# A kernel of eight layer stages on one core: two heads' outputs per column group, one tile for two ternary tails, and a new order of all parts

## The chip, the core and the metric

The kernel runs on one core of a Trainium2 chip, as one program. The metric is the device time of a launch in microseconds. TensorE multiplies, VectorE (DVE) and ScalarE (ACT) do arithmetic and are the only ones that read its results from the accumulation banks, POOL does arithmetic and some DMA issues, and SyncE (SP) issues DMAs. There are eight banks of 128 partitions by 512 fp32 columns.

## What is computed

x has 16 blocks of 128 tokens by 256 features. Eight sub-layers follow one another, each `x = x + f(layernorm(x))`: an attention of 32 heads of 8 dimensions with rotary positions (stage 0 in the code), a product-key expert lookup (1), a grouped attention (2), a routed mixture of experts (3, with 8 and 9 for its tiles), an attention of 16 heads (4), a ternary feed-forward (5), a wide attention of 16 heads of 128 (6) and a feed-forward in blocks of 8-bit numbers (7). The change touches stages 0 and 5:

```
stage 0:  q = rope(x Wq), k = rope(ctx Wk), v = ctx Wv;  P = softmax(q k^T / sqrt(8));  out = (P v) Wout + bout
stage 5:  tern(w) = clip(round(w / s), -1, 1) * s,  s = mean |w|     (w1, w3: 682 x 256, w2: 256 x 682)
          out = (silu(x tern(w1)^T) * (x tern(w3)^T)) tern(w2)^T
```

## The kernel before

All engines work block by block, and several blocks and two stages are under way at once. Each engine's program is a fixed list of parts. `STEPS` names the steps of a stage, how many parts each has per block and which engines take part; `ORDER` (lines 74 to 142) holds for each engine one letter per part, and `timetable` (line 258) turns the letters into the order. `BANKS` says which of the eight banks a step fills; a bank is taken in the order of TensorE's list, and `room` (line 920) makes TensorE wait until the last user of that bank has been read. So the letters and the banks together set who waits for whom.

Stage 0, one block, on TensorE (`small_heads`, line 938; s is 0 for this stage and 4 for the third attention, which shares the code): xT (transpose of the normalised block), qk and vp (projections), tqk (transposes of q and k), mx (four parts: scores, for their row maximum, which VectorE takes at L1881), tq2, st (four parts: transposed scores), pv (eight parts, L1036), tb (L1046), oT (L1053, L1054) and out (L1061, L1062). Scores are products with 32 rows, so they run on quarters of the array. ScalarE takes the exponential of four heads at a time (step ex, L1469) and pv multiplies them by v. v is kept as 32 columns a head in `u0.vt`, of which 8 hold v, one holds 1.0 (its product is the softmax sum) and the others 0.0. The four heads of a part go to four groups of 32 columns of the array, so to four groups of 32 partitions of the bank:

```
h = 16 * (c // 4) + 4 * j + c % 4
r = slice(E * j % 128, E * j % 128 + E)
k = (c - c0) * (E // 32) + E * j // 128
```

Parts 0 to 3 fill bank oa and parts 4 to 7 bank ob. ScalarE copies each out (step ot, L1476, 128x512), TensorE transposes each back in four pieces (step tb, banks ra and rb), and VectorE divides by the sum (step norm, a reciprocal at L1892 and a product at L1896, for 16 heads each). Then oT transposes the 256 features (L1483 on ScalarE copies them) and out multiplies by Wout; VectorE adds to x at L1767. The banks: oa and ra are bank 7; ob and rb are bank 2, which also takes tk. `pv_gone` (line 717) tells ScalarE when a buffer of exponentials is free again.

Stage 5 (`ternary`, line 1252): the weights are turned into -1, 0, 1 in bf16 at the start (step tp on VectorE, L2240 to L2264); x is split into three bf16 parts (step sp), so each product is three. Step h has two parts per block: part 0 fills banks h1 and h3 with tiles 0 to 3 of 128 hidden features, part 1 with tiles 4 and 5, where tile 5 has the last 42 features. Each tile takes 6 products (L1268): 72 in all per block. ScalarE takes silu of h1 (L1635, and L1637 and L1638 for part 1), VectorE multiplies by h3 (L2281, L2284, L2285), the result is split again (step gs) and multiplied by w2 (step out, L1277).

Stage 3's step rk (line 1181) ranks tokens for their expert: `lowh` times this block's marks plus `oneh` times the running sum `seen`, which VectorE writes.

Of the kernel before, what the change touches and what calls it, by code (L numbers as in the profile page):

```python
# [9 lines left out]
BF16 = mybir.dt.bfloat16  # L10
# [3 lines left out]
ALU = mybir.AluOpType  # L14
# [61 lines left out]
        "Zeeaabaababaccdbadbaddfdgdbadhhgdhhgcighfdhhhegdbihgdjhhghkdcaigfdhhhhedbigdahgjhdhkhcigfdhghhdbhgdaihghehdghcjgfdhh"  # L76
        "kdihhegbihdghachjghdkghifdhhhegdibhghadhghcgdjhhhhfikdiebdgahjdghkhgdchgfdhhhhedigibghahhdghjcgdkhhhhfdiiedgbgjhhhdk"
        "ghcgdlhhhhfiidegbdjghhkhgdhcgidlhhhhefidmdgbjghhdhkghdcgilfdhhhhdgiehdgjcdhhghkdgifhdhhhegdihghchjgdhkgdifhhdhhegdih"
        "ghchjgdhkgdifhhdhhgedihghdhjgnhkgfihhhhgoiomghonjhhghhhkigmhhoppiojonokplopmqppnloopomorplnpqpmpooowponwpqrpoopopowp"
        "qrploowomppwnoplqwpowompplonopmqpplnmopoonqoplpoomponolmpnxpqpoopopolqpmpoonopopxqplpomonpooplqpoomopnpopxqplooopmop"  # L80
        "npxqxppwooopxpoqppoossoxpptstopqxptsrspptsuttsqtsrsvuutsvuvvutstsrutsvutsyvutstsvvztstsCuAutsBvutyvzvsutrusCvAtsvruu"
        "BtsvvtuuvysrtzsvuutsAtsvBtsCuvvytzusuvutstsrvCutsAvvuuvttssyutBsrvzuytvCvAusrtuBtsszvuCtsAtvuyvuvBsztyszurvuAtstvutv"
        "vuCsAsytBuvzuBsvCurvAuvtstystBsrtuCtvzusstAtvusvvtuBsyutrsstCtszvutvAuvvuBsyutCszstvuvutvvAusCsytztuBvuAvuvCuBvsstyt"
        "zsusttCvuAvuvvuuBvyuzvuCvvAIBJIIJKJKIyJzIKJIIKJAKCJBDKKEEFEFEFGFEGHFEGHEFEHGFEGFEHHGFEGFEHHGFEGFEHHGFEGFEHHGFEGHFEGH"
        "FEGHFEGFEHHGFEGFEHHGFEGHFEGHFEGFEHHGFEGFEHHGFEGFEHHGFEGFEHHGFEGFEHHGFEGFEHHGFEGFHHGFGHGHGHHIIJJIIKJIKJIKLJIKJOMKJIIK"
        "JKJLKLMOKLMNPNMPQNRQSSSSTPOTLNURMVPQSSSSTORQLTSSTLNUMSSROMVPTLSSLTUNVQPMSSOTRLNSSSSQPTOMTURQUSSVTLNSSROTSSVPTNUQSSPO"
        "MLTRVMUSSLMTLSSOQTVRUNSSLMTPSSNOQPMTZZZZRVNSSQPUTZSSNOTMLRQVSSPSSTNORUTMSSSSQPOTTWWRUQSSVNSSRTONPWSXSTSSQPOXVQRUTTXW"
        "YWXWXWXUSSSSTRXWXYXWSSXYTYSSXVXUTTYVXWXVYUXWXUXWYVXXVXXWYYWXWYXXXXYXXXXW61Y6YXY6XY06Y62062626110-1-1-321321032132415"
        "324154153231421534235241543251342531-41245-450332152-401533724211354253421835014315223424517384525435143224598815+43"
        "2513417501923841528323011234+4557124385984351+424132951527130+843524851432145530129213+13212473578415248403253512435"  # L90
        "891834+5424235597213104+53288403542114232519157321831+48534254234113257507421539881+342541241353251984+3053184715425"
        "4252878793234+5389843754854+8984558+9788+9+9+"),
    "V": (
        "aahabbaababbcaabacbacbaddeebceebaceebaeeaeeeebeecaeedfeeeefeecgeedfieebjeeafeebceegidfjeeeeeebcfeedeegefeicfjeebdeeg"
        "ifeeeefceedeefgeeifeeceegeedyeeeeffceedeegeefeefceegdeejffeeeecgeedfeejfeeeeceegeedfeeeefeedeegeefeeeefdeegeefeeeefd"
# [220 lines left out]
def program(nc, A, out):  # L316
    with ExitStack() as ctx:
# [2403 lines left out]
```

## Time and profile before

| | us |
|---|---|
| median of 3 runs | 2075.73 (2074.39 to 2076.0) |
| the profiled execution | 2073.72 |
| its span, first to last instruction | 2071.8 |
| TensorE busy | 1968.2 (95%) |
| VectorE busy | 1684.7 (81%) |
| ScalarE busy | 1276.6 (62%) |
| granted TensorE clock, mean of the span | 0.990 |

An engine's busy time is the union of its instructions' durations. TensorE's products are pipelined: one has a duration of 0.27 us or so, while the next starts after a part of that, so the mean of a row is a latency and the busy time divided by the count is nearer to its price. PE is the product, PEld the loading of the fixed operand. An fp32 product stands as two records, a transpose as one. Stage 0 lies at about 0 to 240 us, stage 1 to about 590, stage 4 at about 1110 to 1380 and stage 5 at 1297 to 1434.

### The profile page before, as it was taken

What the parts mean: (1) busy time and instruction counts of PE and PEld (TensorE: products, weight loads), DVE (VectorE), ACT (ScalarE), POOL (GpSimd) and SP (SyncE); (2) the same over time, 40 slices, a digit from 0 to 9 for tenths busy, and PEclk for the clock granted to TensorE, in tenths of its full rate; (3) what the DMA queues carried; (4) which work ended last, traced back from release to release, by engine and by line L of the source; (5) the groups of instructions that cost most, each with busy time, mean ns of one, the idle gap of its engine ahead of it and who ended that gap; (6) DMA issues with size and microseconds to landing.
All of it is one profiled execution on the core that took longest, in us unless ns stands there. A gap on an engine that the chain in (4) does not pass through costs nothing.

```text
span 2071.8 us, 46041 instructions
## 1 busy us (share of the span) xinstructions
PE 1968.2 (95%) x16038; PEld 1533.0 (74%) x16038; DVE 1684.7 (81%) x4558; ACT 1276.6 (62%) x3230; POOL 779.6 (38%) x1160
## 2 busy tenths in 40 slices
PE   5999999999999999998998999999899999999998
PEld 3666799899988888887987777887465566555656
DVE  6777899999789997766555788896788988888887
ACT  2778988888855455444654666644666566646661
POOL 7332030000012232222117887022877556646640
PEclk8999999999999999999999999999999999999999
DMA  9400210000045353432211120033667454545540
GB/s 343 140 2 3 78 52 2 2 2 2 13 139 192 113 169 97 133 115 74 91 65 37 29 68 2 2 126 121 223 211 226 133 167 154 186 149 183 170 127 28
DMA packets 223518, 215.75 MB, mean 104 GB/s; under 512 B 25926, under 2 KB 197992, under 8 KB 222264
## 3 DMA queue, kind: packets, MB, share of 16 engines
q1 hardware_dynamic: 197048, 129.17, 20.6%
q0 software_dynamic: 26240, 83.65, 11.2%
q8 instruction: 128, 2.10, 0.4%
q14 instruction: 102, 0.84, 0.1%
HBM read 115.73 MB, written 96.99 MB: 103 GB/s over the span
## 4 chain that ended last, share of the span: by engine, by line
PE 50%; DVE 24%; POOL 8%; issue 7%; DMA 5%; ACT 3%; SPq 3%; DVEq 0%; POOLq 0%; ACTq 0%
PE pb L1135 3%; PE pb L1268 3%; PE pb L1158 3%; PE pb L1107 3%; PE pb L1091 3%; PE pb L1036 3%; PE pb L1009 3%; SPq L873 2%; PE pb L1216 2%; PE pb L1143 2%; PE pb L1150 2%; PE pb L1207 2%; PE pb L1277 2%; PE pb L1100 1%; DMA turn3k<-areaA 1%
## 5 line engine op out<-in xcount | busy, mean ns | idle before, releaser
L2462 POOL TENSOR_SCALAR sm<-sm 128x1 f32<-128x1 f32 x128 | 33.5, 262 | 457.9 <-DVE sm L1752 457.3
L1517 ACT ACTIVATE areaB<-i128h,workB 128x128 f16<-128x128 f16 x512 | 156.3, 392 | 0.9 <-DVE workB L1997 0.6
L1544 ACT ACTIVATE workA<-workA 128x128 f32<-128x128 f32 x256 | 99.5, 390 | 64.0 <-DVE workA L2044 63.8
L1680 ACT ACTIVATE workA<-pb,workA 128x128 f32<-128x128 f32 x256 | 113.8, 457 | 34.5 <-DVE workA L2343 33.0
L1325 PE MATMUL pb<-areaA,workA 128*128 128x256 f32 x512 | 121.7, 382 | 3.8 <-ACT workA L1671 3.7
L1091 PE MATMUL pb<-areaB 128*128 128x128 f32 x1024 | 124.7, 277 | 0.3 <-ACT workB L1507 0.3
L1135 PE MATMUL pb<-xT,areaA 128*128 128x128 f32 x1024 | 124.7, 276 | 0.0
L1135 PEld LDWEIGHTS pb<-xT,areaA 128*128 128x128 f32 x1024 | 119.6, 192 | 5.4 <-issue 5.3
L1469 ACT ACTIVATE areaA<-pb 128x512 f32<-128x512 f32 x192 | 104.9, 603 | 28.7 <-PE pb L1009 28.2
L1325 PEld LDWEIGHTS pb<-areaA,workA 128*128 128x128 f32 x512 | 95.0, 190 | 36.5 <-issue 13.6
L1158 PE MATMUL pb<-areaA,workA 128*128 128x256 f32 x512 | 120.4, 382 | 0.5 <-DVE x L1767 0.5
L1091 PEld LDWEIGHTS pb<-areaB 128*128 128x128 f32 x1024 | 118.1, 192 | 1.8 <-issue 0.6
L2534 POOL DMA_DIRECT2D turn<-workA x64 | 37.0, 579 | 216.1 <-DVE workA L2057 215.9
L1107 PE MATMUL pb<-areaB,workB 128*128 128x256 f32 x512 | 114.1, 381 | 0.8 <-DVE workB L2021 0.8
L1158 PEld LDWEIGHTS pb<-areaA,workA 128*128 128x128 f32 x512 | 93.9, 190 | 18.9 <-issue 6.0
L1107 PEld LDWEIGHTS pb<-areaB,workB 128*128 128x128 f32 x512 | 96.0, 190 | 14.5 <-DVE workB L2021 1.9
L1881 DVE TENSOR_REDUCE workA<-pb 128x4 f16<-128x512 f32 x128 | 82.7, 690 | 20.9 <-PE pb L1009 20.3
L1311 PEld LDWEIGHTS pb<-workA 128*128 128x128 f32 x512 | 64.8, 191 | 39.0 <-ACT workA L1665 20.5
L1009 PE MATMUL pb<-workA 32*128 32x128 f16 (+2 forms) x2048 | 83.8, 255 | 7.5 <-DVE workA L1881 4.1
L2526 POOL TENSOR_TENSOR areaA<-areaA,neghalf 128x32 f32<-128x32 f32 x16 | 88.6, 5540 | 1.3
L1009 PEld LDWEIGHTS pb<-workA 32*128 32x128 f16 (+2 forms) x2048 | 59.7, 142 | 37.2 <-issue 25.4
L1036 PE MATMUL pb<-areaA,workA 128*32 128x128 f32 (+1 forms) x1536 | 81.9, 286 | 4.5 <-ACT areaA L1469 3.7
(421 smaller groups left out, 5790.9 us busy)
## 6 DMA issues: line engine op xcount, KB each, us to landing
turn<-workA POOLq DMA_DIRECT2D x64, 256.0 KB, 2.7
workA<-turn SPq DMA_DIRECT2D x256, 64.0 KB, 2.0
turn3q<-workA POOLq DMA_DIRECT2D x64, 256.0 KB, 2.7
workB<-turn3q SPq DMA_DIRECT2D x256, 64.0 KB, 2.2
turn3k<-areaA POOLq DMA_DIRECT2D x64, 256.0 KB, 2.8
workA<-turn3k SPq DMA_DIRECT2D x256, 64.0 KB, 2.2
turn3p<-areaA POOLq DMA_DIRECT2D x64, 256.0 KB, 2.7
rows_in<-areaB SPq DMA_DIRECT2D x7, 2048.0 KB, 16.8
```

Of the source, the lines that this page charges most:

```text
L1009: m = eng.matmul(p[k][:, j * 128:(j + 1) * 128], one, two, start=True, stop=True)
L1036: m = eng.matmul(p[r, k * 128:(k + 1) * 128], vt[:, h, :], P[:, j * 128:(j + 1) * 128], start=True, stop=True)
L1091: m = eng.matmul(p[:, e * 128:(e + 1) * 128], w.ed[:, k, (4 * c + e) * 128:(4 * c + e + 1) * 128], xT[:, k, :], start=(k == 0), stop=(k == 1))
L1107: m = eng.matmul(p[:, 0:256], G[:, e, :], w.eu[:, e, :], start=(e == 0), stop=(e == 15))
L1135: m = eng.matmul(p[:, h * 128:(h + 1) * 128], w.wq[:, 4 * c + h, k], xT[:, k, :], start=(k == 0), stop=(k == 1))
L1158: m = eng.matmul(p[:, 0:256], u.OT[i][:, h], w.wo[:, 4 * c + h], start=(c == 0 and h == 0), stop=(c == 3 and h == 3))
L1325: m = eng.matmul(p[:, 0:256], u.OT[i][:, h], w.wo[:, 4 * c + h], start=(c == 0 and h == 0), stop=(c == 3 and h == 3))
L1469: eng.activation(u.P[n % RP], bank(s, tag, b, at)[:, :], ACT.Exp, scale=1.0 / math.sqrt(hd)).then_inc(freed(s, tag, b, at)[0], 1)
L1517: m = eng.activation(u.far[:, g], i128h[:, :], ACT.Square, bias=u.at[b % 2][:, 8 * c + g:8 * c + g + 1])
L1544: m = eng.activation(u.P[i][:, h], u.P[i][:, h], ACT.Exp, accum_out=u.den[i][:, h:h + 1], bias=u.nm[i][:, h:h + 1])
L1680: m = eng.activation(u.P[i][:, h], p[:, h * 128:(h + 1) * 128], ACT.Exp, accum_out=u.den[i][:, h:h + 1], bias=u.nb[i][:, h:h + 1], scale=u ...
L2526: eng.tensor_tensor(va, va, neghalf[:, 0:32], ALU.pow).then_inc(S["l2_rs"], 1)
```

## The change

Stage 0: heads c and c+4 of a group of columns share its 32 rows. v of heads 16 to 31 is moved 16 columns on (`vset`), so that their product fills rows 16 to 24 of the group and adds 0.0 to the rows of the other head. One bank o (bank 7) takes all eight parts, with one start and one stop, then one ot, one tb (bank r, number 2) and one norm per block. `Wout` comes with its rows in the new order of heads. Stage 4 keeps two banks. Stage 5: w3's columns are rolled by 42, so w1's tail, 22 columns of zeros and w3's tail stand side by side, and one tile of 106 columns gives both tails in bank h3. In stage 3, rk waits also for the last write of `seen`. The order of all parts on all engines is new: TensorE has 1885 parts for 1901, VectorE 2209 for 2225, ScalarE 1559 for 1575, POOL 735 and SyncE 360 as before.

```diff
-        ("ex", 8, "A"), ("pv", 8, "T"), ("ot", 2, "A"), ("tb", 2, "T"), ("norm", 2, "V"), ("oT", 1, "TA"),
+        ("ex", 8, "A"), ("pv", 8, "T"), ("ot", 1, "A"), ("tb", 1, "T"), ("norm", 1, "V"), ("oT", 1, "TA"),
...
-    (0, "pv"): lambda b, c: {0: (("oa", 7),), 4: (("ob", 2),)}.get(c, ()),
-    (0, "tb"): lambda b, c: ((("ra", 7),), (("rb", 2),))[c],
+    (0, "pv"): lambda b, c: (("o", 7),) if c == 0 else (),
+    (0, "tb"): lambda b, c: (("r", 2),),
...
-        u0.OTs = [carve(1024) for _ in range(2)]
+        u0.OTs = [carve(512) for _ in range(2)]
+        u0.O = [carve(256) for _ in range(2)]
...
-        u0.vt = [carve(1024).rearrange("p (h e) -> p h e", e=32) for _ in range(RV)]
-        u0.O = [carve(256) for _ in range(2)]
+        u0.vflat = [carve(1056) for _ in range(RV)]
+        u0.vt = [ap[:, 0:1024].rearrange("p (h e) -> p h e", e=32) for ap in u0.vflat]
+        u0.vset = [ap.rearrange("p (a n) -> p a n", a=2)[:, :, 0:512].rearrange("p a (h e) -> p a h e", e=32) for ap in u0.vflat]
...
+            if s == 0:
+                return full(0, "o", b) if c == 7 else (S["l0_pvd"], nth(b, c, 7))
...
-                        k = (c - c0) * (E // 32) + E * j // 128
+                        k = c % 4 if s == 0 else (c - c0) * 2 + j // 2
                         m = eng.matmul(p[r, k * 128:(k + 1) * 128], vt[:, h, :], P[:, j * 128:(j + 1) * 128],
-                                       start=True, stop=True)
+                                       start=(s == 4 or c == 0), stop=(s == 4 or c == 7))
...
+                elif step == "tb" and s == 0:
+                    t.wait_ge(*freed(0, "o", b))
+                    p = room(0, "r", b)
+                    for k in range(4):
+                        m = eng.transpose(p[:, k * 128:(k + 1) * 128], u.OTs[b % 2][:, k * 128:(k + 1) * 128], ident)
+                    m.then_inc(full(0, "r", b)[0], 1)
...
+                elif step == "ot" and s == 0:
+                    a.wait_ge(*full(0, "o", b))
+                    if b >= 2:
+                        a.wait_ge(*full(0, "r", b - 2))
+                    eng.copy(u.OTs[b % 2], bank(0, "o", b)[:, :]).then_inc(freed(0, "o", b)[0], 1)
...
-                    eng.reciprocal(rec.unsqueeze(3), ov[:, :, :, 8:9]).then_inc(*v.mark())
+                    eng.reciprocal(rec, ov[:, :, 8:9]).then_inc(*v.mark())
...
-                    eng.tensor_tensor(Oi, ov[:, :, :, 0:8], bc(rec, 3, [128, 4, 4, 8]), ALU.mult).then_inc(freed(0, tag, b, c)[0], 1)
+                    eng.tensor_tensor(O, ov[:, :, 0:8], bc(u.rec, 2, [128, 32, 8]), ALU.mult).then_inc(freed(0, "r", b)[0], 1)
...
+                    if b > 0:
+                        t.wait_ge(S["m_pos"], b)
...
-                    for tag, wm in (("h1", w.w1), ("h3", w.w3)):
+                    both = (("h1", 0), ("h3", 746))
+                    for tag, at in both:
                         p = room(5, tag, b, c)
-                        for m_ in range(4 if c == 0 else 2):
-                            mt = 4 * c + m_
-                            M = 42 if mt == 5 else 128
+                        tiles = [(128 * m_, at + 128 * (4 * c + m_), 128) for m_ in range(4 if c == 0 else 1)]
+                        if c == 1 and tag == "h3":
+                            tiles.append((128, 640, 106))
+                        for to, n0, M in tiles:
...
-                        eng.activation(u.a[1][0:42, 128:256], p[0:42, 128:256], ACT.Silu,
+                        a.wait_ge(*full(5, "h3", b, c))
+                        eng.activation(u.a[1][64:106, 128:256], bank(5, "h3", b, c)[0:42, 128:256], ACT.Silu,
...
+                    eng.memset(w.w13[:, :, 682:704], 0.0)
```

## Rows read from the trace of the kernel before

**Rows 1.** The page, part 1: busy us, share of the span, instructions.
```profile
PE 1968.2 (95%) x16038; PEld 1533.0 (74%) x16038; DVE 1684.7 (81%) x4558; ACT 1276.6 (62%) x3230; POOL 779.6 (38%) x1160
```
**Rows 2.** Windows view of TensorE: start:end, length, busy (instructions), clock, DMA share, GB/s.
```profile
0.00:52.00 52.00, 29.38 (x214) 0.89 1.01 343
52.00:220.00 168.00, 165.24 (x2614) 0.98 0.14 44
220.00:250.00 30.00, 25.12 (x323) 0.94 0.07 19
250.00:500.00 250.00, 246.65 (x2647) 1.00 0.08 26
...
1300.00:1440.00 140.00, 140.00 (x1714) 1.00 0.20 70
1440.00:2072.00 632.00, 593.55 (x2275) 1.00 0.52 165
```
**Rows 3.** Chain of waits from 52 to 220 us, shares by engine and line.
```profile
by line: PE pb L1036 18.6%; PE pb L1009 18.3%; PE pb L1046 8.7%; PE pb L983 7.4%; PE pb L971 4.9%; PE pb L1061 4.7%; PE pb L1017 3.9%; PE pb L956 3.4%; PE pb L1062 3.3%; issue 2.7%; PE pb L957 2.6%; PE pb L959 2.6%; ACT areaA L1469 2.5%; PE
```
**Rows 4.** Windows view of VectorE, then of ScalarE.
```profile
52.00:220.00 168.00, 129.61 (x307) 0.98 0.14 44
250.00:500.00 250.00, 241.28 (x1081) 1.00 0.08 26
1300.00:1440.00 140.00, 114.83 (x302) 1.00 0.20 70
...
52.00:220.00 168.00, 129.47 (x237) 0.98 0.14 44
```
**Rows 5.** Groups by line, 60 to 220 us: busy us, mean ns, idle before.
```profile
L1435 ACT COPY workA<-pb 128x1024 f16<-128x1024 f16 x27 | 27.6, 1023 | 0.9 <-PE pb L983 0.7 <-PE pb L1017 0.2
...
L1046 PE MATMUL pb<-cst,areaA 128*128 128x128 f32 x116 | 18.1, 281 | 0.0
L1476 ACT COPY areaA<-pb 128x512 f32<-128x512 f32 x28 | 17.0, 606 | 5.8 <-PE pb L1036 5.7
...
L1896 DVE TENSOR_TENSOR workA<-pb,areaA 128x128 f32<-128x128 f32 x29 | 8.5, 292 | 1.0
...
L1892 DVE RECIPROCAL areaA<-pb 128x16 f32<-128x16 f32 x29 | 7.2, 249 | 4.3 <-PE pb L1046 4.2
...
L1767 DVE TENSOR_TENSOR x<-x,pb 128x256 f32<-128x256 f32 x14 | 5.8, 415 | 2.6 <-PE pb L1062 2.4
...
L959 PEld LDWEIGHTS pb<-areaA,ctxT 128*128 128x128 f32 x20 | 3.8, 190 | 0.5
```
**Rows 6.** Timeline, 120 to 134 us: start us, us, engine, line, tiles.
```profile
128.47 0.65 PE L1046 MATMUL pb<-cst,areaA 128*128 128x128 f32 x4
...
128.96 0.60 PE L956 MATMUL pb<-areaA,xT 128*128 128x256 f32 x2
```
**Rows 7.** POOL's memsets (line view), then the longest wait at the start.
```profile
L2476 POOL MEMSET workA<- x4: 952/972/1006, 4.5 to 943.5; 128x1024 f32 x4
...
PE pb L971 <- DMA areaA<-in_L_xattn_Wkv: 8.2, 1, 8.2
```
**Rows 8.** Waits from 60 to 220 us: us in total, times, longest.
```profile
ACT areaA L1469 <- PE pb L1009: 21.5, 29, 1.8
...
PEld pb L1009 <- issue: 14.8, 61, 0.4
```
**Rows 9.** Ternary product: groups, 1290 to 1440 us, then timeline.
```profile
L1268 PEld LDWEIGHTS pb<-workB,areaB 128*128 128x128 bf16 x960 | 55.0, 98 | 4.5 <-issue 1.1 <-DVE workB L1775 0.2
...
L1268 PE MATMUL pb<-workB,areaB 128*42 128x128 bf16 x192 | 16.4, 221 | 0.0
...
L1268 PEld LDWEIGHTS pb<-workB,areaB 128*42 128x42 bf16 x192 | 11.0, 100 | 3.3
...
1402.75 8.96 PE L1268 MATMUL pb<-workB,areaB 128*128 128x128 bf16 x144
```
**Rows 10.** DMA issues, 1290 to 1450 us: count, KB each, us to landing.
```profile
areaA<-in_L_xattn_Wo SPq DMA_DIRECT2D x2, 1024.0 KB, 13.2
```

More of the change, by code:

```diff
@@ L80 @@
[L80 to L83, printed above, removed]
@@ L587, in program @@
         w5.tmp = carve(1364)
-        w5.sign = carve(2132).bitcast(BF16)
-        w5.w1 = w5.sign[:, 0:1364].rearrange("p (k n) -> p k n", k=2)
-        w5.w3 = w5.sign[:, 1364:2728].rearrange("p (k n) -> p k n", k=2)
-        w5.w2 = w5.sign[:, 2728:4264].rearrange("p (k n) -> p k n", k=6)
+        w5.sign = carve(2154).bitcast(BF16)
+        w5.w13 = w5.sign[:, 0:2772].rearrange("p (k n) -> p k n", k=2)
+        w5.w1, w5.w3 = w5.w13[:, :, 0:682], w5.w13[:, :, 704:1386]
+        w5.w2 = w5.sign[:, 2772:4308].rearrange("p (k n) -> p k n", k=6)
+        w5.places = (w5.w1, w5.w3, w5.sign[:, 2772:4052], w5.sign[64:106, 4052:4308])
         carve = carver(work[1])
@@ L1021, in small_heads @@
                 elif step == "pv":
-                    tag, c0 = ("oa", "ob")[half], half * (ng // 2)
+                    tag, c0 = ("o", 0) if s == 0 else (("oa", "ob")[half], 2 * half)
                     if c == c0:
@@ L1459, in small_heads @@
                     if b >= RV:
-                        a.wait_ge(*full(0, "ob", b - RV, 4))
-                    eng.copy(u.vt[b % RV][:, :, 0:8], bank(0, "v", b)[:, 0:256].rearrange("p (h e) -> p h e", e=8)
+                        a.wait_ge(*full(0, "o", b - RV))
+                    eng.copy(u.vset[b % RV][:, :, :, 0:8], bank(0, "v", b)[:, 0:256].rearrange("p (a h e) -> p a h e", a=2, e=8)
                              ).then_inc(freed(0, "v", b)[0], 1)
@@ L2257, in ternary @@
                     q = min(j, 2)
-                    r, m, sign = raw[0:rows, lo:hi], w.tmp[0:rows, 0:hi - lo], w.sign[0:rows, lo:hi]
+                    r, m, sign = raw[held[j], lo:hi], w.tmp[held[j], 0:hi - lo], w.places[j]
+                    if j < 2:
+                        r, m = (ap.rearrange("p (k n) -> p k n", k=2) for ap in (r, m))
                     v.settle()
@@ L2261, in ternary @@
                         v.wait_ge(S["t_q"], j)
-                    eng.tensor_scalar(m, r, sm[0:rows, 8 + q:9 + q], None, ALU.is_gt).then_inc(*v.mark())
+                    eng.tensor_scalar(m, r, sm[held[j], 8 + q:9 + q], None, ALU.is_gt).then_inc(*v.mark())
                     v.settle()
-                    eng.scalar_tensor_tensor(sign, r, sm[0:rows, 12 + q:13 + q], m, ALU.is_lt, ALU.subtract).then_inc(S["t_q"], 1)
+                    eng.scalar_tensor_tensor(sign, r, sm[held[j], 12 + q:13 + q], m, ALU.is_lt, ALU.subtract).then_inc(S["t_q"], 1)
                 elif step == "sp":
@@ L2475, in small_heads @@
                     for k in range(RV):
-                        m = eng.memset(u.vt[k], 0.0)
+                        m = eng.memset(u.vflat[k] if s == 0 else u.vt[k], 0.0)
                     m.then_inc(*g.mark())
@@ L2683 @@
     a["mask"] = a["maskT"].T.reshape(2048)
+    a["wo0"] = I["L0_xattn_Wout"].reshape(2, 4, 4, 8, 256).transpose(2, 1, 0, 3, 4).reshape(256, 256)
     a["edT"] = I["L0_ffn_e_down"].T
```

167 lines of the change are left out of this document (86 added, 81 removed), and 4 rows, old and new, of the table TAKEN.

## The prediction

> **What bounds the kernel now.** I read the page first. TensorE is busy for 1968 of 2072 us, VectorE for 1685, ScalarE for 1277 [rows 1]. That is a mean, so the second view is TensorE's busy time by stage [rows 2]. Of its 104 us of idle time, 22.6 lie in the first 52 us (weights and first blocks) and 38.5 after 1440 us, where the last attention goes through memory for its transposes; the rest is spread over the stages between. The two places that the change touches are almost gap-free: 165.2 of 168 us in the first attention (52 to 220 us), 140.0 of 140 in the ternary feed-forward (1300 to 1440 us). So an instruction taken off TensorE there is worth its own time, unless another engine is just behind. The third view is the chain of work that ended last, cut to the first attention [rows 3]: it runs over TensorE's lines one after the other, with L1046 (the transposes of step tb) at 8.7%, and the first other engine in it has 2.5%. Between 250 and 500 us, in the expert lookup that follows, VectorE is just behind: it is busy for 241.3 us of 250 [rows 4]. That stretch could take back what the first one gives.
>
> **Head outputs (first attention).** Before, eight steps pv write one product per head into two banks, of which each head uses 9 of its 32 rows. Now heads c and c+4 of a column group share the 32 rows. The number of products stays. One bank in place of two has to be copied, transposed and normalised, so each of 16 blocks loses one ot copy, one tb step of four transposes and one norm.
> - TensorE, removed: 64 of 128 transposes. By busy time one is 18.1/116 = 0.156 us [rows 5], 10.0 us in all. By the chain it is less, since neighbours overlap: 8.7% of 168 us is 14.6 us for the 29 tb steps (116 transposes) that [rows 5] count, so 0.50 us a step and 8.1 us for 16. The start times say the same: one tb from 128.47 to the next product at 128.96 is 0.49 [rows 6], 7.8 for 16. Ends 7.8 and 10.0; I take 8.1, the chain's own.
> - ScalarE, removed: 16 copies of 0.606 us, 9.7 us [rows 5]. It is busy 129.5 of 168 us there [rows 4]. Nothing on the path; it makes room.
> - VectorE, removed: 16 reciprocals (0.249) and 16 products (0.292); the others double their width, so the product goes from 0.292 to about 0.415, the time of a 128x256 sum from a bank at L1767, and the reciprocal to 0.25 to 0.5 [rows 5]. Net per block 1.08 minus 0.67 to 0.92: 3 to 7 us in all. VectorE is at 129.6 of 168 [rows 4], so again nothing at once.
> - Added: bank 7 is now filled over all eight pv and is free only after the one copy. Before its turn for tb, TensorE needs the product's own 0.28 (the mean of a transpose, the nearest row), the copy's 0.61 [rows 5] and a hand-over, about 1.0 us. By the new order the work between the last pv and tb, priced as the timeline spaces such steps (0.5 for tq2, mx and st, 0.43 for vp), is 0.5 to 2.7 us, median 1.43; two blocks (9 and 14) have only 0.5. Two others have 0.5 between tb and oT, where the norm (about 1.0) must fit. About four stalls of 0.4: plus 1.5 us. Zero if the copy starts early, the rival below if it starts late.
> - Moved buffers: u0.O to the other area, vt from 1024 to 1056 columns. The first costs nothing; the second adds 3% to two memsets of 0.972 us [rows 7] while TensorE waits for the first weights anyway (8.2 us [rows 7]). The row order of Wout is permuted in memory; same load.
>
> A rule that bears on this: each tb stands between products on 32-column or 32-row tiles. The trace shows TensorE's loads at L1009 idle 14.8 us in 61 places for no releaser, 0.24 us each [rows 8]. The Trainium skill (TensorEngine Tiling (Array Packing), Key Properties) says that changing the tiling mode drains the engine; by it each removed tb could also remove such a gap, and the sum would be deeper by up to 3.9 us. I don't add it: the 0.49 above already runs to the next product's start.
>
> **Ternary tails.** Before, 682 columns of each matrix end in a tile of 42, so a block issues 72 products; now both tails lie in one tile of 106 columns, 66 products. 96 of 1152 go. Pace: 144 products in 8.96 us are 0.062 each [rows 9], and nothing stands idle in this stretch. Minus 5.9 us. Bounds: by the busy time of the 42-wide form (16.4/192) 8.2 us [rows 9]; nothing, if the wider tile's load stood in the way. A 42-column load takes 100 ns and a 128-column one 98 [rows 9], so 106 columns should take the same. The Trainium skill (TensorE: Matmul & The Clock Gate, Weight-path perf modes) grants fast loading only to 128 columns and prices other loads by their columns; as an estimate that makes 106 columns 88 ns against 35 for 42, and the sum would be 5.1 us worse. The row for 42 columns already contradicts it.
> ScalarE's silu of the tail now waits for the h3 bank too, which TensorE fills 12 products, some 0.74 us, after h1. Behind it on ScalarE stand the next block's xT copy and the casts that VectorE's splits need; at worst 0.74 for each of 16 blocks, but TensorE works blocks ahead here, so I take 0. VectorE is busy 114.8 of 140 us there [rows 4] and keeps its work; 4% less on TensorE leaves it the slower of the two. Setup: one memset of 44 columns on VectorE before the absolute sums, under the 0.292 of a 128x128 sum [rows 5], beside the third attention. The last weights come back to partitions 64 to 105; same load.
>
> **Order and waits.** All queues are ordered anew. Counting parts ahead of each stage's end: TensorE has 2 queries, 4 of g and no am of the lookup in front of the end of the first attention, where it had 3, 7 and 2; VectorE one top-k chain where it had two; POOL's and SP's orders shift by a few places. Before, TensorE lost 4.9 us between 220 and 250 us [rows 2]; the new order keeps about as much work (27.5 against 29.5 us by paces) between the first similarities and the first am, so that loss stays. The last output of stage 4 stands about 35 us of TensorE work ahead of stage 6's first product in either order, more than the 13.2 us landing of its slowest weights [rows 10]. The new wait in rk costs nothing: in the new VectorE order the mark of a block always follows the previous block's rk. Elsewhere I take 0 for the reordering, with 4 us either way: idle time to win or lose is 38.5 us in the last stretch.
>
> **Sum.** Minus 8.1, plus 1.5, minus 5.9: minus 12.5 us. The profiled execution took 2073.72 (span 2071.8 and 1.9 around it), the median shown is 2075.73, 2.0 above. 2075.7 minus 12.5 is **2063.2**. A measurement of this kernel can tell about 0.2% (4.2 us) from no change; faster means under 2071.6.
>
> **Rivals.**
> 1. VectorE takes the first saving. If the lookup is bound by VectorE, its end moves only with VectorE's start and remaining work: the first similarities come 2.2 us earlier by the new order, and 2.4 us less first-attention work is left on VectorE behind them, so 4.6 in place of 8.1 us. For it: 241.3 of 250. Against: TensorE is at 246.7 in the same stretch [rows 2]. With little back from the tails 2075.7 - 4.6 - 4 = 2067. Chance 0.2.
> 2. Wider gain: the drained switches go with the tb steps (3.9 us) and the new order wins another 4 us of idle time: 2055. Chance 0.13.
> 3. Slower: the single copy comes late. On ScalarE the new order puts ot behind a tqk copy (1.02 us [rows 5]) and the last ex (0.60). If both are still ahead when the last pv ends, TensorE waits 0.28 + 1.62 + 0.61 = 2.5 us against 1.43 of cover, 1.1 per block, 17 us; with a wait of the next block's pv on bank 7 as well, another 0.6 per block, 10 us. That gives 2075.7 - 14 + 27 = 2089. It turns the sign from 0.9 us per block on. Against: ScalarE has 23% idle, and waits 21.5 us itself for products [rows 8]. Chance 0.06.
> 4. The change does nothing much: the saved instructions were overlap, and later waits on memory in the last stretch take the rest (TensorE 593.5 of 632 us there). 2074. Chance 0.09.
> 5. The 106-column tile is dear: between 100 ns and the 190 of a full-width fp32 load [rows 5], 8.6 us if nothing hides it: 2072. Chance 0.03.
> The forecast itself, 2059 to 2067: 0.49.
>
> **How the numbers follow.** Faster: forecast, rivals 1 and 2 and a little of 4: 0.84. Same: most of 4 and 5: 0.10. Slower: 0.06. The range leaves out rival 3 and half of 4: 2052 to 2072.
>
> **What would show it.** Right: L1046's successor with 64 fewer records and 16 fewer ot copies; TensorE busy about 1950 us; the first attention's end 8 us earlier; the ternary product with 1056 records at 0.062, and its stretch 6 us shorter. Wrong: new idle time of TensorE ahead of tb or of the first pv with ScalarE's ot as its releaser; VectorE at over 98% between 250 and 500 us; loads of 106 columns well over 100 ns; the gain of 14 us visible at 1440 us and gone by the end.

## The result and the profile after

The changed kernel takes **2095.63 us** (median of 4 runs, 2094.58 to 2097.32), against 2075.86 for the kernel before in the same job (a job is a set of kernels whose executions were timed together): ratio 1.0099, 95% interval 1.0083 to 1.0115. It is slower by 1%, where 2063 was forecast. The profiled execution spans 2095.5 us against 2071.8.

The page of the changed kernel, part 1, beside [rows 1]:

```profile
PE 1968.6 (94%) x15878; PEld 1528.4 (73%) x15878; DVE 1688.6 (81%) x4527; ACT 1263.5 (60%) x3208; POOL 780.6 (37%) x1160
```

160 products and transposes are gone, as planned, and TensorE is busy as long as before, where some 1950 us was expected. So the time must be read by stage. A "stand" below is a stretch in which an engine is idle. TensorE's windows of the changed kernel, beside [rows 2]:

```profile
0.00:52.00 52.00, 33.07 (x202) 0.93 1.01 355
52.00:220.00 168.00, 160.15 (x2595) 1.00 0.12 41
220.00:250.00 30.00, 26.26 (x322) 1.00 0.64 219
250.00:500.00 250.00, 241.53 (x2576) 0.99 0.01 2
500.00:900.00 400.00, 398.86 (x2911) 1.00 0.36 116
900.00:1150.00 250.00, 228.74 (x1581) 0.96 0.23 71
1150.00:1300.00 150.00, 133.99 (x1495) 0.93 0.11 33
1300.00:1440.00 140.00, 135.49 (x1862) 1.00 0.16 54
```

Against before, idle time is new in the first attention (5 us), in the lookup (from 3.4 to 8.5 us in 250 to 500) and, with a granted clock of 0.93 where it was 1.00, in the third attention (16.0 us idle from 1150 to 1300, 10.4 before). The removed work itself is there. The transposes of the first attention from 60 to 220 us, and the ternary product with its weight loads:

```profile
L1050 PE MATMUL pb<-cst,areaA 128*128 128x128 f32 x56 | 9.1, 285 | 0.1
...
L1285 PE MATMUL pb<-workB,areaB 128*128 128x128 bf16 x960 | 59.5, 219 | 1.3 <-DVE workB L2310 0.8 <-DVE areaA L1933 0.4
L1285 PE MATMUL pb<-workB,areaB 128*106 128x128 bf16 x96 | 8.0, 219 | 0.0
...
L1285 PEld LDWEIGHTS pb<-workB,areaB 128*128 128x128 bf16 x960 | 55.1, 98 | 4.9 <-issue 1.7 <-DVE workB L2310 1.5 <-DVE areaA L1933 0.7
L1285 PEld LDWEIGHTS pb<-workB,areaB 128*106 128x106 bf16 x96 | 6.5, 128 | 0.0
```

1056 records as expected. A load of 106 columns takes 128 ns, longer than one of 128 (98) and one of 42 (100 in [rows 9]).

**One stand of the last stretch can be read to its cause.** TensorE's timeline of the changed kernel near 2064 us, then VectorE's (start, duration, what it waited for in brackets):

```profile
2060.65 3.62 PE L1381 MATMUL pb<-areaB,workB 128*128 128x256 f32 x16
2067.18 0.45 PE L939 MATMUL pb<-cst,areaB 128*128 128x128 f32 x1 [2.92 <-DVE x L1790]
2067.42 0.42 PE L940 MATMUL pb<-cst,areaB 128*128 128x128 f32 x1
2068.31 2.07 PE L1364 MATMUL pb<-areaB,workB 128*128 128x512 f32 x2 [0.46 <-ACT workB L1427]
2070.17 1.91 PE L1365 MATMUL pb<-areaB,workB 128*128 128x512 f32 x2
2071.88 1.84 PE L1364 MATMUL pb<-areaB,workB 128*128 128x512 f32 x2
2073.56 1.02 PE L1365 MATMUL pb<-areaB,workB 128*128 128x512 f32 x2
```

```profile
2065.48 1.23 DVE L2389 TENSOR_TENSOR workB<-workB 128x1024 f32<-128x1024 f32 x1
2066.62 0.41 DVE L1790 TENSOR_TENSOR x<-x,pb 128x256 f32<-128x256 f32 x1
```

L1381 is the output product of feed-forward block 12, in PSUM bank 0; L939 are the transposes of block 15, which go into the same bank. The product ends at 2064.3, but the new order gives VectorE the quantising step `ha` of block 14 first (3.1 us, its last instruction here L2389), and only then the sum at L1790 that empties the bank. TensorE stands 2.92 us, and behind it each pair of 512-column products takes 1.8 to 2.1 us in place of 1.02: the granted clock is 0.53 of full speed from 2067 to 2074 us. In the old order the product comes one step earlier, and VectorE takes it ahead of `ha`.

### The profile page after: what moved, and what is told of

Same layout as the page of the kernel before. It is cut to its first block, busy times and chain, and to the rows that moved or that the text cites. A ratio compares the mean times of both kernels' runs of the same rounds, so it can differ in the third digit from the quotient of the medians.

```text
span 2095.5 us, 45664 instructions
## 1 busy us (share of the span) xinstructions
PE 1968.6 (94%) x15878; PEld 1528.4 (73%) x15878; DVE 1688.6 (81%) x4527; ACT 1263.5 (60%) x3208; POOL 780.6 (37%) x1160
## 4 chain that ended last, share of the span: by engine, by line
PE 45%; DVE 31%; POOL 10%; issue 7%; ACT 3%; DMA 2%; SPq 1%; DVEq 0%; another core or an unknown queue 0%; POOLq 0%; ACTq 0%
PE pb L1148 5%; PE pb L1171 5%; PE pb L1013 3%; PE pb L1156 3%; PE pb L1163 3%; PE pb L1040 2%; PE pb L1120 2%; PE pb L1104 2%; POOL workA L2587 2%; POOL workA L2593 2%; PE pb L1231 2%; POOL workA L2599 1%; PE pb L1222 1%; DVE workB L1952 1%; PE pb L1285 1%
## 5 line engine op out<-in xcount | busy, mean ns | idle before, releaser
L1171 PEld LDWEIGHTS pb<-areaA,workA 128*128 128x128 f32 x512 | 94.1, 190 | 22.6 <-issue 10.1
L1040 PE MATMUL pb<-areaA,workA 128*32 128x128 f32 (+1 forms) x1536 | 87.4, 286 | 4.5 <-ACT areaA L1486 4.3
L1328 PEld LDWEIGHTS pb<-workA 128*128 128x128 f32 x512 | 65.5, 191 | 33.4 <-issue 25.5
```

The lines of the kernel that those rows point to most:

```text
L1040: m = eng.matmul(p[r, k * 128:(k + 1) * 128], vt[:, h, :], P[:, j * 128:(j + 1) * 128], start=(s == 4 or c == 0), stop=(s == 4 or c == 7))
L1171: m = eng.matmul(p[:, 0:256], u.OT[i][:, h], w.wo[:, 4 * c + h], start=(c == 0 and h == 0), stop=(c == 3 and h == 3))
```

## The experiments

18 kernels, in four jobs after the one above. All ratios are to the kernel before in the same job; "clock" is the mean, over the runs of a kernel, of span times (1 - granted clock), the most that stretches at 1.2 GHz can cost. It counts such a stretch in full even where TensorE stands in it and loses nothing. For the kernel before it is 21 to 24 us in these four jobs, for the changed kernel it was 30.9 in the first one.

| kernel | edits | order | ratio, 95% | clock, us |
|---|---|---|---|---|
| both_old_order | both | old | 0.9989, 0.9972 to 1.0006 | 28.5 |
| tails_only | tails | old | 0.9978, 0.9966 to 0.9991 | 25.2 |
| heads_only | heads | old | 1.0023, 1.0010 to 1.0037 | 30.5 |
| new_then_old | both | new to 1125 us, old | 1.0019, 1.0008 to 1.0030 | 25.1 |
| old_then_new | both | old to 1119 us, new | 0.9999, 0.9985 to 1.0013 | 25.5 |
| new_old_tail | both | new, last 140 us old | 1.0034, 1.0020 to 1.0048 | 23.0 |
| after_again | both | new | 1.0063, 1.0042 to 1.0084 | 26.4 |
| after_two_swaps | both | new but two places | 1.0030, 1.0016 to 1.0045 | 22.0 |
| old_new_old | both | old, new 1119 to 1928 us, old | 0.9980, 0.9966 to 0.9995 | 25.8 |
| old_lookup | both | old to 590 us, new, last 140 us old | 0.9991, 0.9977 to 1.0006 | 25.3 |
| new_lookup | both | new to 592 us, old | 1.0043, 1.0026 to 1.0059 | 28.8 |
| no_heads_mid | tails | as old_new_old | 1.0000, 0.9987 to 1.0014 | 20.9 |
| before_padded | none, 16 idle products | old | 1.0040, 1.0026 to 1.0055 | 21.2 |
| heads_padded | heads, 16 idle products | old | 1.0012, 0.9995 to 1.0029 | 22.6 |
| heads_refilled | heads, 32 idle products | old | 1.0055, 1.0040 to 1.0069 | 21.4 |
| after_filled | both, 64 idle products | new | 1.0107, 1.0083 to 1.0132 | 16.2 |
| tails_filled | tails, 73 idle products | old | 1.0043, 1.0030 to 1.0056 | 8.7 |
| mid_filled | both, 32 idle products | as old_new_old | 0.9986, 0.9973 to 0.9999 | 12.8 |

**Edits or order.** The order tables are plain text, so the change can be taken apart. For the first two kernels below the new strings of `ORDER` give way to the old ones (less the dropped parts where the heads edit is in); this is the first line of TensorE's:

```diff
-        "eeZabaabaabaccdbadbaddfdgdbdhaghchdghhhgfdhhegdibahgdjhhghkhdgchhhedfidjgbdahghkhgdchghfdhhhedgibadhghjhdghkchghfdhh"
+        "Zeeaabaababaccdbadbaddfdgdbadhhgdhhgcghfdhhhegdbihgdjhhghkdcagfdhhhhedbigdahgjhdhkhcgfdhghhdbhgdaihghehdghcjgfdhhkdh"
...
```

> Both edits with the order of the kernel before (only the dropped parts removed from it: the first tb, ot and norm of each block). Theory O (the new order costs, the edits gain): 14 us below the kernel before, 2062. Rival S (the edits themselves cost, through the one long-held bank or the wide tile): at or above 2090, like the changed kernel. Rival N (order and edits only fit together badly: the old order was laid out for the old durations): between 2070 and 2080.

> The kernel before with the ternary tile of 106 columns alone, order unchanged. By the step of the prediction (96 products of 0.062): 6 us less, 2070. If the wide tile or silu's later start costs: no gain. If the saved time is given back before the last attention's weights and transposes: 1 to 3 us less.

For heads_only the ternary part of the diff is left out of that kernel as well (and the heads part of it for tails_only):

```diff
-                    both = (("h1", 0), ("h3", 746))
+                    for tag, wm in (("h1", w.w1), ("h3", w.w3)):
...
```

> The kernel before with the shared head rows and the one bank alone, in the old order less the dropped parts. By the step of the prediction (16 tb steps of 0.50, some stalls): 6.6 to 8 us less, 2068. If the expert lookup behind it is bound by VectorE: 4 to 5 us less. If the one bank stalls TensorE: at or above 2076.

The two edits in the old order are worth 2 us, not 12.5, and with 1.0000 inside the interval no gain is shown at all: the tails give 4.5 us of gain, the heads 4.8 us of loss. And the order costs 1.1% (0.9989 to 1.0099; by a later job of the same changed kernel 0.7%), the larger part of the miss. The new wait in rk is in both_old_order and in neither of the single edits, whose ratios would make 1.0001 together; so it shows no cost.

**Which part of the order.** The queues were cut at one time in all five, each taking the parts that had started by then from one order and the rest from the other. For new_then_old:

```diff
-        "FEGFEHHGFEGFEHHGFEGFEHHGFEGFEHHGFEGFEHHGFEGFEHHGFEGFEHHGFEGFEHHGFGFHHGGHHGIHJIIJKJKIIJIKJIKLJKOMKJIIJKJLKKOMLLMNPNMP"
+        "FEGFEHHGFEGFEHHGFEGFEHHGFEGFEHHGFEGFEHHGFEGFEHHGFEGFEHHGFEGFEHHGFGFHHGGHHGIHJIIJKJKIIJIKJIKLJKOMKJIIJKJLKLMOKLMNPNMP"
...
```

> Both edits; the new order up to the start of the third attention (the first 1142 of TensorE's 1885 parts and the same cut on the others), then the old order for all that is left. Theory O with its place (the third attention's new order loses 22 us, the part before it ends 6 us late): 2062 + 6 to 10 = 2068 to 2072. If the loss sits in the first half or is spread: 2080 or more.

> Both edits; the old order up to the start of the third attention (the first 1119 us), the new order from there. Theory (the loss of the change sits in the new order from the third attention on, about 0.8%, and adds to what precedes it): 1.0070 of before, some 2090 us, 16 us above the same edits in the old order throughout (2073.6). Rival (the second half of the new order is only bad because the first half of the new order delivers its blocks in another rhythm; each half alone is harmless): 1.000, 2076 us.

The halves cost 0.3% and 0.1%, together they should cost 0.4%, and the whole costs 1.1%: both of my theories fell, new_then_old's (2068 to 2072 us, measured 2081) and old_then_new's (1.0070). Next the last 140 us alone went back; TensorE's lines of it:

```diff
-        "5274130+53284843501242135921715+138213435284254131257437540352918+183425142435135291+4835701438154224552988743273+53"
-        "983+4885748459845589+7889++9+"),
+        "5274130+53284843501242135921715+138213435284254131257437540352918+18342541241353251984+30531847154254252878793234+53"
+        "89843754854+8984558+9788+9+9+"),
...
```

> The changed kernel, with the order of its last 140 us alone put back (TensorE's last 73 of 1885 parts, and what stands beside them on the other engines). In the changed kernel TensorE stands 2.9 us at 2064 us for the residual sum of the last block, with a stretch at half clock behind it (6.8 us, so 3.4 us lost). Theory (this is one of the places where the new order loses): 6 us less than the changed kernel, 1.0070, 2090 us. Rival (that stall only stands for time that another place would cost anyway): within 2 us of the changed kernel, 1.010.

0.65% less, twice what the last stretch could give. Its profile shows where the rest came from: the third attention, whose order is the same in both: in the two profiles the last product of the stage before it (expert work, stage 9) ends at 1124.4 us in the changed kernel and 1123.1 in new_old_tail, and the third attention's own last product at 1406.0 and 1391.6. So the changed kernel was run again, without an edit (its diff is empty):

> The changed kernel once more, unchanged, beside the next ones on one chip, for a second profile of it. Putting back the order of its last 140 us alone took 0.65% off (1.0099 to 1.0034), though that stretch had only 6 us to give: in the first profile of the changed kernel the third attention too was 6 us longer than in the kernel with the old tail, with no difference in its order, and VectorE and ScalarE stood there 4 us together (1226 to 1231 us) for nothing that the profile shows. Theory A (that stand was a mishap of one execution, and the time of the changed kernel hangs on chance in the third attention): the second profile has no such stand, and the ratio here is 1.005 to 1.007. Theory B (it belongs to the kernel): the stand comes at the same place again, ratio 1.010.

1.0063 (1.0042 to 1.0084), and the second profile has no such stand: theory A. With this ratio the order costs 0.7%, and the 0.4% of the two halves is within the error of it. TensorE from 1150 to 1300 us, first the changed kernel's profile, then the same kernel's second one:

```profile
1150.00:1200.00 50.00, 44.59 (x490) 0.91 0.10 28
1200.00:1250.00 50.00, 43.97 (x487) 0.93 0.16 49
1250.00:1300.00 50.00, 45.43 (x527) 0.93 0.06 22
```

```profile
1150.00:1200.00 50.00, 44.80 (x532) 0.97 0.10 28
1200.00:1250.00 50.00, 46.91 (x541) 1.00 0.22 70
1250.00:1300.00 50.00, 45.75 (x595) 1.00 0.01 2
```

The two longest waits in the first one, 1220 to 1235 us (TensorE's longest there is 3.1 us, for VectorE); "remote" is the profile's word for a releaser that it does not see:

```profile
DVE workA L1906 <- remote: 4.9, 1, 4.9
ACT workA L1456 <- remote: 4.7, 1, 4.7
```

Then the two places alone that the timeline above blames:

```diff
-        "983+4885748459845589+7889++9+"),
+        "983+488574845984558+97889++9+"),
...
-        "{/%9+{/}=-!$<-*>=9=<+*>/9-<*+9>/%+{=/(((()<[]>=9{}<+!>--$/9-*+*/{{}=-!=$%<*<(((()>=*[]{><%=><{}!>{${}!${()[]{}%!${{}"
+        "{/%9+{/}=-!$<-*>=9=<+*>/9-<*+9>/%+{=/(((()<[]>=9{}<+!>--$/9-*+*/{{}=-!=$%<*<(((()>=*[]{><%=><{}!>{${}!${()[]{%}!${{}"
```

> The changed kernel with two places of its order put back: TensorE does the output product of feed-forward block 12 before the transposes of block 13, and VectorE takes that product before its 3.1 us GELU step of block 14 (in the changed kernel after it). The product lies in PSUM bank 0, which the transposes of block 15 need next, so TensorE stands 2.9 us at 2064 us, and runs 6.8 us at half clock behind it. Theory: stand and slow stretch go, 4 to 6 us less than the changed kernel beside it, and the rest of the gain of the old tail is elsewhere. Rival (these two places make the whole difference of the old tail): 13 us less, 1.0034.

1.0030 beside after_again's 1.0063: 6.9 us for moving one letter in each of two strings, and as much as putting back the whole tail (1.0034). The bank that VectorE emptied too late is shown to cost this: a stand of 2.92 us, and some 3 us of the slow clock behind it.

For old_new_old and the two lookup cuts the first line of each queue is the old one or the new one, as above, and the change of order falls inside; TensorE's string of old_new_old begins and ends with the old lines:

```diff
-        "eeZabaabaabaccdbadbaddfdgdbdhaghchdghhhgfdhhegdibahgdjhhghkhdgchhhedfidjgbdahghkhgdchghfdhhhedgibadhghjhdghkchghfdhh"
+        "Zeeaabaababaccdbadbaddfdgdbadhhgdhhgcghfdhhhegdbihgdjhhghkdcagfdhhhhedbigdahgjhdhkhcgfdhghhdbhgdaihghehdghcjgfdhhkdh"
...
-        "983+4885748459845589+7889++9+"),
+        "89843754854+8984558+9788+9+9+"),
```

> Both edits; old order to the start of the third attention, new order through the third attention, the ternary stage and most of the rest, old order again for the last 140 us. The kernel with the new order from the third attention to the end was 0.9999 of before, and its last stretch had the same 6 us stand and slow clock as the changed kernel. Theory (the two losses are apart, the tail costs 6 us wherever it stands): 0.997, some 2063 us where before is 2070, the fastest with both edits. Rival (gains at the tail were already lost by chance elsewhere): 0.9999.

0.9980, 4 us less than old_then_new, as the tail's stand would have it, though the two intervals overlap. The rest of the loss then lies in the first 1119 us (1.0030 with the new beginning, 0.9980 with the old). The last two runs cut that at the lookup's end:

> Both edits; old order up to the end of the lookup (590 us), new order from there to 1938 us, old order for the end. With the new order from the start and an old end it was 1.0030 to 1.0034, with the old order up to 1119 us 0.9980. Theory (the loss of the first part sits in the first attention and the lookup): 0.998, 4 us faster than before. Rival (it sits behind 600 us, in the second attention, the routing and the experts): 1.003.

> Both edits; new order up to the end of the lookup (592 us), old order from there to the end. The old order throughout was 0.9989. Theory: 1.003 to 1.004, 6 to 8 us slower than before. Rival: 0.999.

These two kernels differ behind 590 us as well, so each is set beside the one that shares its later order: new_lookup's 1.0043 beside both_old_order's 0.9989, 11 us, and old_lookup's 0.9991 beside new_old_tail's 1.0034, 9 us. So 0.4 to 0.5% sits in the first attention and the lookup. The profiles agree: the lookup's last product ends at 583.4 us in old_lookup and at 594.7 in new_lookup, with the same number of products of every stage issued by then. TensorE in the profiles of old_lookup and then of new_lookup, windows and the longest waits from 225 to 600 us:

```profile
225.00:300.00 75.00, 74.72 (x820) 0.97 0.27 89
300.00:400.00 100.00, 98.98 (x1079) 1.00 0.01 2
400.00:600.00 200.00, 198.24 (x2004) 1.00 0.11 34
...
PE pb L1086 <- DVE x L1790: 1.4, 1, 1.4
PE pb L1113 <- DVE workB L2033: 0.9, 1, 0.9
```

```profile
225.00:300.00 75.00, 67.72 (x725) 0.93 0.26 89
300.00:400.00 100.00, 99.60 (x1070) 1.00 0.01 2
400.00:600.00 200.00, 196.70 (x2044) 1.00 0.07 20
...
PE pb L1113 <- DVE areaB L2033: 3.3, 4, 2.1
PE pb L1104 <- ACT workB L1529: 3.3, 2, 3.0
PE pb L1086 <- ACT areaB L1427: 1.8, 2, 1.4
```

The new stands are at the beginning of the lookup, 225 to 300 us: 7.3 us idle in place of 0.3, with VectorE and ScalarE as the releasers. The new order ends the first attention sooner (its last product at 229.4 us, not 241.5, with 130 of the lookup's 3584 products ahead of it, not 262) and leaves less of it to mix in, so that TensorE has nothing to do while the other two work through the first blocks of the lookup. That is not the whole loss: 3 us of idle time are saved before 225 us and 1 us more is lost behind 300, so by the lookup's end the new order has 39.2 us idle in place of 34.2. The other 6.4 of the 11.4 us are busy time, the same products taking longer, with as much time at the slow clock in both (23.9 us); which neighbours cost it no run separates.

**What a microsecond of the first attention is worth.** `keep_busy` puts products of no use ahead of a part:

```diff
-FILL = {}
+FILL = {(0, "tb", b, 0): 2 for b in range(16)}
```

> The heads edit alone in the old order (1.0023 of before, 4.8 us slower, although its first attention ends 3.7 to 6 us earlier), with two products of no use (0.43 us) ahead of each of the 16 transpose steps, about what the four dropped transposes took (0.50 us). Theory (the saving of the first attention is real but worth nothing, since the third attention gives it back with interest when it starts earlier): no slower than the edit alone, 1.000 to 1.002, and the first attention ends as late as before. Rival (TensorE's time in the first attention is worth what it is, and the edit's new waits cost on top): 1.004 to 1.006, 4 to 7 us slower than the edit alone.

Two such products are four passes of 0.215 us, 0.86 us ahead of each step, where the four dropped transposes took 0.50. So 14 us were put in, not 7, for 6.6 us of time, and that the rival's number came is no support for it. With one product in place of two, in the old and in the new form:

```diff
-FILL = {}
+FILL = {(0, "tb", b, 0): 1 for b in range(16)}
```

> The kernel before with one product of no use (0.43 us) ahead of the first transpose step of each of the 16 blocks of the first attention: 6.9 us more of TensorE's time there, nothing else. Theory A (a microsecond of the first attention is a microsecond of the whole): 1.0033, 7 us slower. Theory B (the stages from 900 to 1240 us give back most of a lead or a lag, as heads_refilled's 12.5 us at 230 us had become 4.9 us at 1240): 1.0005 to 1.0015, 1 to 3 us slower.

> The heads edit alone in the old order, with one product of no use (0.43 us) ahead of each of its 16 transpose steps, so that TensorE has within 1.5 us as much to do in the first attention as before; what is left of the edit is its waits. Theory A (a microsecond there counts in full): 1.0023 + 0.0033, 1.0056. Theory B (most is given back): 1.003, and so the waits of the edit, not its missing work, make its loss: heads_padded over before_padded is 4 to 6 us in both.

8.3 us for 6.9 us of work in the old form: theory A. In the new form 6.9 us more of work cost nothing (1.0023 to 1.0012), which neither theory has (1.0056, 1.003). With the products in both forms the edit gains 5.8 us (1.0040 to 1.0012), without them it loses 4.8. The clock column has most of the difference: heads_only loses 7.3 us more to the clock than before, heads_padded 1.1. In the profiles the difference is made in the third attention, which the edit does not touch: between the first transposes of its block 8 and its scores of block 8 heads_only takes 61.6 us, before, before_padded, heads_padded and heads_refilled 57.0 to 57.1; both_old_order, which has the heads edit without products too, takes 60.8. The profiled execution of heads_only is the shortest of its twelve, so it shows less than the usual loss. TensorE's timeline of heads_only there, then before's:

```profile
1214.36 0.69 PE L1022 MATMUL pb<-cst,workA 128*128 128x128 f32 x4 [2.04 <-DVE workA L1901]
1215.31 1.98 PE L1039 MATMUL pb<-areaA,workA 128*64 128x128 f32 x16 [0.26 <-ACT areaA L1503]
1217.22 2.09 PE L1012 MATMUL pb<-workA 16*128 16x128 f32 x32
```

```profile
1216.54 0.66 PE L1019 MATMUL pb<-cst,workA 128*128 128x128 f32 x4 [1.14 <-DVE workA L1884]
1217.13 1.09 PE L1036 MATMUL pb<-areaA,workA 128*64 128x128 f32 x16
```

A stand of 1.14 us has become one of 2.04, and the same sixteen products behind it take 1.98 us in place of 1.09.

**Can the clock be had back?** Products of no use where TensorE stands:

```diff
-FILL = {}
+FILL = {(4, 'tqk', 0, 0): 3, (4, 'mx', 0, 0): 5, (4, 'tqk', 1, 0): 5, (4, 'tqk', 2, 0): 8,
+        (4, 'vp', 2, 0): 8, (4, 'pv', 5, 0): 4, (4, 'tq2', 7, 0): 11, (4, 'qk', 14, 0): 9,
+        (7, 'xT', 15, 0): 11}
```

> The changed kernel, with products of no use (64 in all, 0.215 us each at full clock) in nine places ahead of parts for which TensorE stood 0.9 to 3.1 us, each some 80% as long as the stand was: eight in the third attention, one at 2064 us. Nothing else waits less. Theory (of the 17 us that the new order of the third attention costs, half is the stands themselves, and half that TensorE's clock falls to 1.2 GHz behind them): the five slow stretches of 6.8 us from 1134 us on mostly go, the stands stay, so 8 to 17 us less than the changed kernel, 2079 to 2087 us, mean granted clock 0.991 or more against 0.985. Rival (the clock falls for other reasons, and the products stand in the way): no less than the changed kernel, 2095 to 2105, clock 0.985.

For tails_filled the same in eleven places, the longest of them:

```diff
+        (8, 'tT', 0, 0): 22, (4, 'tqk', 0, 0): 3, (4, 'mx', 0, 0): 5, (4, 'tqk', 1, 0): 4,
```

> The ternary tails alone in the old order (0.9978 of before), with products of no use in eleven places where TensorE stood: four in the first 45 us, one ahead of the experts' first tile (5 us long), six in the third attention's first blocks. Theory of the clock: most of the five to six slow stretches (24 us lost per run, by the mean granted clock of 0.988) go, so 8 to 15 us less than without them: 0.991 to 0.994, 2057 to 2064 us, and this is the fastest of all. Rival (the stands are what costs): the same as without them, 0.998, or slower by the products that come late.

Both were twice as long as meant, by the mistake of 0.215 for 0.43 us, and neither gained: after_filled 1.0107 (changed kernel 1.0063 and 1.0099) with the clock column at 16.2, tails_filled 1.0043 (tails_only 0.9978) with 8.7. So the clock rose and the rivals hold, but with 28 and 31 us of products in stands meant for half of that. With the right length:

```diff
-FILL = {}
+FILL = {(0, "qk", 2, 0): 3, (0, "tqk", 0, 0): 3, (0, "mx", 0, 3): 4, (0, "tq2", 0, 0): 2, (8, "tT", 0, 0): 11,
+        (4, "tqk", 0, 0): 1, (4, "mx", 0, 0): 2, (4, "tqk", 1, 0): 2, (4, "tqk", 2, 0): 2, (4, "st", 1, 0): 2}
```

> old_new_old (both edits, 0.998) with 32 products of no use (0.43 us each, 14 us in all) in ten places where TensorE stood 0.9 to 6 us, never more than 0.8 of the stand. The granted clock was 0.9875 there (25.8 us lost per run). Theory of the clock: stretches at 1.2 GHz near 27, 41, 966, 1126 and 1136 us go, lost time falls to 10 to 14 us, and the time by 6 to 12 us: 0.992 to 0.995. Rival (products of no use delay the work behind the stand by as much as the clock gives): clock 0.993, time 0.997 to 1.001.

The clock does as expected: 12.8 us lost in place of 25.8, and 1.00 in the first 52 us. TensorE in mid_filled, then in old_new_old:

```profile
0.00:52.00 52.00, 29.41 (x245) 1.00 1.00 338
900.00:1150.00 250.00, 234.74 (x1670) 0.98 0.22 71
```

```profile
0.00:52.00 52.00, 29.67 (x234) 0.87 1.01 340
900.00:1150.00 250.00, 226.79 (x1632) 0.96 0.22 69
```

The time does not: 0.9986 beside 0.9980. The rival holds. The 13 us were not 13 us of work: in the first 52 us TensorE is busy for 29.4 and 29.7 us, at either clock. At the lookup's last product mid_filled is 3.7 us behind (586.1 us, not 582.4), with 5.2 us of products put in by then, and by the end it has made that up. How much of it the clock paid back no run separates.

Last, old_new_old's order under the tails alone, in the kernel before's own steps (two of tb, ot and norm a block; the new wait in rk is in it), a line of VectorE's queue as the example of what it takes over:

```diff
-        "YWXWXWXUSSSSTRXWXYXWSSXYTYSSXVXUTTYVXWXVYUXWXUXWYVXXVXXWYYWXWYXXXXYXXXXW61Y6YXY6XY06Y62062626110-1-1-321321032132415"
+        "WSWSYXXWXXUXWXWTXSSYTVRXSSYYXSSYXWXUXWTTVYXWXUXYVXUYWXWXVYVXYXXXYXWXYXWXYXXYXY6160Y6626062626011--1-1321323102134251"
...
```

> The ternary tails alone (0.9978 in the old order), with the new order's middle (from the third attention to 1924 us) between old beginning and old end. Theory (the middle of the new order is worth 1 to 3 us, as old_new_old's 0.9980 against 0.9989 for both edits in the old order): 0.9965 to 0.9975, the fastest of all. Rival (the middle fits only the kernel for which it was found): 0.998 to 1.000.

1.0000: the rival, and a warning about the small differences in this table. The middle of the new order helped the kernel for which it was searched and not its neighbour.

## Why the prediction was wrong

**The order, costed at nothing, is the step that failed.** "Elsewhere I take 0 for the reordering, with 4 us either way" has to read plus 15 to 23 us: from both_old_order to after_again 0.7%, to the first job's changed kernel 1.1%. Shown by runs: 9 to 11 us up to the end of the lookup (5 of them idle time, net) and 7 us for one bank at 2064 us. Both places were within reach of reading. For the first I compared how much lookup work stood ahead of the first attention's end, found less of it (2 queries, 4 of g and no am), and wrote that "that loss stays"; the same count says that less of the first attention is left to fill the lookup's first blocks, whose work waits for VectorE, busy 96% in [rows 4]. For the second, only L1790's place in VectorE's queue against the next user of bank 0 had to be looked up; I counted parts ahead of stage ends and never bank reuse in the tail. The 38.5 us of idle time in the last stretch were named as what could be won or lost and priced at 4 us either way; one bank alone cost 7.

**The heads edit: the term was right, its worth was not.** The transpose step went from 17.0 to 8.6 us of TensorE's time over the first attention (heads_only beside before, each transpose counted from the end of the work ahead), so 8.4, where 8.1 was taken from the chain [rows 3]. That 8.1 set the chain from 52 us against the 29 steps counted from 60 us; from 52 us there are 30, which makes 7.8. The new stands were under-sized: TensorE's idle time in the first attention rose by some 4 us in heads_only, ahead of steps mx, tq2, st and oT, with VectorE's row maximum (L1898) and ScalarE's copy of the queries (L1447) as the chief releasers, where 1.5 us ahead of tb was forecast. Ahead of tb itself stood 0.2 us; rival 3, the late single copy, fell. And what was won there, 3.7 to 6 us at 230 us, was kept through the lookup (so rival 1 fell too, in the old order) and lost in the third attention to a stand and the clock behind it. With the same products added to both forms the edit is worth 5.8 us, close to the 6.6 forecast; as made it costs 4.8. Why the third attention falls one way or the other is shown only as far as the timeline goes: a stand of 2.04 us in place of 1.14.

**The ternary tails: more work saved, less time.** Two blocks of products took 8.96 us for 144 [rows 9] and take 7.54 for 132 in tails_only's timeline, so 0.71 us a block, 11 us in all, where 5.9 was taken. The pace of 0.062 was a mean over unlike products. In the trace of before a product of 42 columns behind one of 128 starts 149 ns after it (all 32 times), one of 128 columns directly behind one of 42 starts 152 ns after it (20 times), and the others mostly 56 ns; with 106 columns it is 56 ns into such a product, between two and out of one. So the edit took out 96 products of 0.056, 5.4 us, and with them these 52 changes of width at some 94 ns, 5 us. But from the start of the first of these products to the end of the stage's last output product tails_only needs 134.1 us where before needs 135.6: 1.4 us. TensorE's waits in tails_only from 1290 to 1440 us, where before had none:

```profile
PE pb L1280 <- DVE workB L1779: 2.9, 2, 2.7
PE pb L1054 <- DVE x L1771: 1.8, 2, 1.3
PE pb L1271 <- DVE workB L2293: 1.3, 2, 0.8
```

VectorE is at 118 of 140 us there, and "4% less on TensorE leaves it the slower of the two" was too quick: it has room on the mean and none where the third attention's end and the ternary blocks meet. The measured 4.5 us of the edit come close to the forecast 5.9, but three of them come from elsewhere and may be chance. The step on the load of 106 columns was wrong by itself: "106 columns should take the same" as 42 and 128, and it takes 128 ns against 98 and 100. The rule of the Trainium skill that I set aside (TensorE: Matmul & The Clock Gate, Weight-path perf modes), fast loading for 128 columns alone, has this row on its side and the 42-column row against it. The longer load cost nothing: the products start 56 ns apart with either width.

**Busy time as a sign.** "TensorE busy about 1950 us" failed though the work went: 1968.6 with 160 instructions fewer. Products at half clock last twice as long and count as busy (8 us more are lost to the clock than before), and so do products that follow each other less closely, as the 6.4 us above.

**The range.** Of 2052 to 2072 neither the changed kernel's 2095.6 nor the edits in the old order (0.9989, 2073) came inside, since it gave a new order on all five engines less width than the 7 and 9 to 11 us that two places of it cost. Rival 3's 2089 was nearest in number, by luck: its late copy did not happen.

## What to carry to other kernels

A re-ordered schedule is a change of its own, with a price of its own: run the old order with the new code first, and read the new one for two things, a PSUM bank whose emptying stands behind a long step of another engine, and a stage's beginning that lost the neighbour's work that used to fill it. Two letters moved gave back 0.3% here; the best of these kernels (old_new_old, 0.9980, and tails_only, 0.9978) take only part of the change. In a kernel whose engines hand over every microsecond, an edit of 5 us is as easily turned round by a stand and its clock 1000 us later as it is kept: time it beside padded forms before believing its sign.

## What the runs showed of the hardware

- Most of the scatter of one kernel goes with TensorE's clock. both_old_order spans 2065.3 us at a mean granted clock of 0.990 and 2080.7 at 0.983; 0.007 of the span is 14.5 of the 15.4 us between them. Span times clock scatters by 2.6 us (standard deviation of 12 runs), the span by 4.6.
- Products of no use in TensorE's stands raise the clock from 0.9875 (old_new_old) to 0.994 (mid_filled) and gain no time (0.9980 and 0.9986).
- A weight load of 106 columns (bf16) takes 128 ns, one of 128 columns 98.
- A change between bf16 products of 128 and of 42 columns costs 93 to 96 ns (starts 149 and 152 ns apart, not 56); between 128 and 106 columns it costs nothing (56).
- Once, VectorE (4.9 us) and ScalarE (4.7 us) stood together near 1226 us with no releaser in the profile, and TensorE 3.1 us for VectorE. It was not there in the second profile of the same kernel. That job's four runs of the changed kernel were at 1.0099 and the later job's six at 1.0063; whether such stands make that difference stays open.
